# Blocked attention with one score pass: queries on partitions, exponentials turned by TensorE, divisors as extra value columns

## What is computed

```python
# x = x + att(layernorm(x)); 16 heads of 8 features, blocks of 32 tokens
qkv = (x @ Wqkv.T)                      # 128 -> 3 * 128
q, k = rope(q), rope(k)
att = einsum('bhnqd,bhnkd->bhnqk', qb, kb) * 8 ** -0.5   # within a block of 32 only
att = where(causal, att, min)
att = softmax(att, axis=-1)
out = einsum('bhnqk,bhnkd->bhnqd', att, vb)
return out.reshape(...) @ Wout.T
```

## Time and profile before

| | |
|---|---|
| time of the runs | 3553.87 us median of 3 (3552.51 to 3564.93) |
| span of the profiled execution | 3553.8 us, its own time within 0.1 us of the median |
| TensorE busy | 2772.3 us, 78% |
| VectorE busy | 2182.0 us, 61% |
| ScalarE busy | 1794.2 us, 50% |
| GpSimd busy | 1143.1 us, 32% |
| mean granted clock of TensorE | 0.844 of 2.4 GHz |

### The profile page before, as it was taken

The page is one execution under the profiler, slowest core; times in us unless marked ns, Lnnn a source line. Parts: engine busy times, 40 slices in busy tenths (PEclk is TensorE's granted clock), DMA queues, the critical chain, the costliest instruction groups (busy, mean ns, idle before and its releaser), DMA issues. The chain is left out here.

```text
span 3553.8 us, 75251 instructions
## 1 busy us (share of the span) xinstructions
PE 2772.3 (78%) x28949; PEld 2193.2 (62%) x28949; DVE 2182.0 (61%) x8175; ACT 1794.2 (50%) x3540; POOL 1143.1 (32%) x1567
## 2 busy tenths in 40 slices
PE   6788887659588585359489999999999668548886
PEld 3466664447366454246378888888888545336665
DVE  6566647753357733444477777777777663464546
ACT  5244435224234332236368988889897444313332
POOL 3200004440642613656552222222222265650002
PEclk9699978779678787669799999999999778757776
DMA  9200000015100143115100000000000014310000
GB/s 278 80 3 3 3 2 1 18 49 143 46 20 2 36 118 100 44 57 179 43 19 12 8 5 12 12 1 12 12 1 1 5 39 140 104 29 3 4 4 25
DMA packets 134083, 148.41 MB, mean 42 GB/s; under 512 B 14817, under 2 KB 109922, under 8 KB 133730
## 3 DMA queue, kind: packets, MB, share of 16 engines
q1 hardware_dynamic: 106306, 71.13, 6.9%
q0 software_dynamic: 27424, 72.48, 6.8%
HBM read 77.63 MB, written 65.93 MB: 40 GB/s over the span
## 5 line engine op out<-in xcount | busy, mean ns | idle before, releaser
L202 PE MATMUL bank<-ident,xn 128*128 128x128 f32 x320 | 72.6, 368 | 327.2 <-DVE xn L190 168.3
L2766 POOL TENSOR_SCALAR shared_floats<-shared_floats 128x2 f32<-128x2 f32 x256 | 57.2, 224 | 720.0 <-DVE shared_floats L2757 719.9
L2688 PE MATMUL bank<-layer,shared_floats 128*128 128x128 f32 x2048 | 278.2, 280 | 0.0
L1798 PE MATMUL bank<-shared_floats 32*128 32x32 f32 (+4 forms) x2048 | 222.1, 344 | 62.7 <-DVE shared_floats L1943 35.1
L202 PEld LDWEIGHTS bank<-ident,xn 128*128 128x128 f32 x320 | 47.6, 185 | 346.2 <-DVE xn L190 172.2
L2045 ACT ACTIVATE shared_floats<-bank 128x480 f32<-128x480 f32 (+2 forms) x256 | 104.5, 460 | 306.9 <-PE bank L1819 306.8
L2688 PEld LDWEIGHTS bank<-layer,shared_floats 128*128 128x128 f32 x2048 | 256.5, 197 | 0.0
L2999 ACT ACTIVATE shared_floats<-bank,layer 128x256 f32<-128x256 f32 x512 | 210.1, 470 | 89.8 <-PE bank L2675 89.7
L2675 PE MATMUL bank<-shared_floats,layer 128*128 128x256 f32 x1024 | 242.9, 380 | 0.0
L1943 DVE TENSOR_REDUCE shared_floats<-bank 128x2 f32<-128x256 f32 (+3 forms) x320 | 134.8, 471 | 170.5 <-PE bank L1812 169.8
L1805 PE MATMUL bank<-shared_floats 32*128 32x32 f32 (+7 forms) x2048 | 232.2, 339 | 4.5 <-ACT shared_floats L2045 2.4
(11 more groups left out here) (355 smaller groups left out, 8552.3 us busy)
## 6 DMA issues: line engine op xcount, KB each, us to landing
bins<-zero SPq DMA_DIRECT2D x1, 18176.0 KB, 86.6
shared_floats<-bins SPq DMA_DIRECT2D x32, 320.0 KB, 4.2
results<-shared_floats SPq DMA_DIRECT2D x32, 320.0 KB, 3.5
expert_weights<-in_dram_experts SPq DMA_DIRECT2D x32, 312.0 KB, 3.1
layer<-in_dram_layers SPq DMA_DIRECT2D x8, 902.0 KB, 4.7
bins<-zero SPq DMA_DIRECT2D x1, 5760.0 KB, 22.4
bins<-xn,f_bin_row POOLq DMA_INDIRECT x256
results<-results,result_rows POOLq DMA_INDIRECT x128
```

Source lines behind the costliest of these rows:

```text
L1798: T.matmul(k.bank[4 + r % 2][:, at_a:at_a + wide_a], q_heads[rows32(r), blk * P:(blk + 1) * P], kk[rows32(r), half_a * BK + begin_a:half_a ...
L2688: m = T.matmul(to, hidden[:, n * S + t * P:n * S + (t + 1) * P], w["w2"][:, tile(n)], start=False, stop=(n == NF - 1), skip_group_check=True)
```

## The change

`att3_*` no longer share code with `att0_*`. There is one score pass: the queries of a block are the stationary operand (32 rows by 32 columns), the spread keys the moving one (128 columns, four heads by 32 keys), so a batch's scores for all 16 heads lie with queries on partitions in two banks (`pair_of_banks`, banks 4 and 5 or 6 and 7 by turns). VectorE takes the maximum of every 32 columns and subtracts it (`shift`), ScalarE takes the exponentials of 1024 columns, TensorE turns them with eight transposes into the same two banks (`turn_exps`), ScalarE copies them (`copy_turned`), and `weigh` uses them as the stationary operand (32 columns) with the values as the moving one, 36 columns: the last four hold ones for the head's own keys (`same_head`), so that the divisor comes out of the same matmul. The result has tokens on partitions and is turned by two transposes (`turn_att`, `copy_att`) before the output projection. Queries are no longer spread. Chunks are normalised two ahead. Keys are projected before queries. The eight banks become slices of one PSUM tensor.

```diff
-BLOCKED_A = [[(b, b * BK, b * BK + BK) for b in range(BLOCKS)]]
-BLOCKED_ORDER = [("score", 0, 0), ("project", 0, 0), ("heads", 0, 0), ("weigh", 0, 3), ("divide", 0, 3), ("stats", 0, 0),
...
-BLOCKED = Softmax("L3_wqkvT", BLOCKED_A, BLOCKED_B, 4, 3, BLOCKED_ORDER, CAUSAL)
+V_WIDTH = BK + 4
+def pair_of_banks(k, n):
+    first = 4 + n % 2 * 2
+    return k.banks[:, first * CH:(first + 2) * CH]
+def heads_at(r, t):
+    return slice(r % 2 * CH + r // 2 * S + t * P, r % 2 * CH + r // 2 * S + (t + 1) * P)
 def att3_tensor(k, s):
-    softmax_tensor(k, s, BLOCKED)
+    def score(n):
+        c, to = n // 2, pair_of_banks(k, n)
+        q, _, k_heads, _ = att3_buffers(k, c)
...
+        for bank in range(2):
+            T.matmul(tiles(to[:, bank * CH:(bank + 1) * CH], BK), k.ident_bf[:, :],
+                     k.w["masks"][:, MASKS["ahead_a"]][:, 0:BK].unsqueeze(1).broadcast_to([P, CH // BK, BK]),
+                     start=True, stop=False, skip_group_check=True)
+        for rows in ((0, 1), (2, 3)):
+            if rows[0]:
+                T.wait_ge(k.sem("at_max"), LEFT["at_max"] + n + 1)
+            for t in range(QT):
+                for b in range(4):
+                    blk = n % 2 * BLOCKS + t * 4 + b
+                    for r in rows:
+                        m = T.matmul(to[rows32(b), heads_at(r, t)], q[rows32(r), blk * BK:(blk + 1) * BK],
+                                     k_heads[rows32(r), blk * P:(blk + 1) * P], start=False, stop=True, skip_group_check=True)
+            m.then_inc(k.sem("at_scored_a" if rows[0] else "at_max"), 1)
+    def turn_exps(n):
...
+        for r in range(4):
+            for t in range(QT):
+                m = T.transpose(to[:, heads_at(r, t)], exps[:, heads_at(r, t)], k.ident[:, :])
+    def weigh(n):
...
+        for t in range(QT):
+            for r in range(4):
+                for b in range(4):
+                    at = ((n % 2 * BLOCKS + t * 4 + b) * 4 + r) * V_WIDTH
+                    m = T.matmul(k.bank[3][rows32(b), (t * 4 + r) * V_WIDTH:(t * 4 + r + 1) * V_WIDTH],
+                                 turned_exps[:, heads_at(r, t)][:, b * BK:(b + 1) * BK],
+                                 v_heads[:, at:at + V_WIDTH], start=True, stop=True, skip_group_check=True)
...
+    for n in range(B + 1):
+        c, odd = n // 2, n % 2
+        on, more = n < B, c + 1 < NC
+        if on:
+            score(n)
+        if on and not odd:
+            values(c, 0)
+            values(c, 1)
+        if n:
+            weigh(n - 1)
+        if on and not odd:
+            values(c, 2)
+            values(c, 3)
+            if more:
+                ln_turn(k, s, c + 1)
+        if on and odd and more:
+            project(c + 1, 0)
+        if on:
+            turn_exps(n)
+        if n:
+            turn_att(n - 1)
+        if on and not odd and more:
+            project(c + 1, 1)
+        if n:
+            project_out(n - 1)
 def att3_vector(k, s):
-    softmax_vector(k, s, BLOCKED)
+    def shift(n):
...
+        v.count(V.tensor_reduce(tops[:, :], scores, AX.X, ALU.max))
...
+        V.tensor_tensor(tiles(exps[:, :], BK), scores, tops[:, :].unsqueeze(2).broadcast_to([P, 4 * BLOCKS, BK]),
+                        ALU.subtract).then_inc(k.sem("at_shifts_made"), 1)
+    def divide(n):
...
+        v.count(V.reciprocal(by_heads, sums[:, :, BK:V_WIDTH]))
...
+    for n in range(B + 1):
...
+        if on:
+            shift(n)
+        if n:
+            divide(n - 1)
+        if on and not odd and c + 2 < NC:
+            ln_stats(k, s, c + 2)
+        if on and not odd and more:
+            turn_heads(c + 1, 1)
+        if on and odd and more:
+            turn_heads(c + 1, 0)
+        if on and odd and c + 2 < NC:
+            ln_apply(k, s, c + 2)
+        if n:
+            add_out(n - 1)
 def att3_scalar(k, s):
-    softmax_scalar(k, s, BLOCKED)
+    for n in range(B + 1):
...
+        if on and not odd:
+            copy_values(c, 0)
+            copy_values(c, 1)
+        if on:
+            exps(n)
+        if on and not odd:
+            copy_values(c, 2)
+            copy_values(c, 3)
+            if more:
+                ln_copy(k, s, c + 1)
+        if on and odd and more:
+            mask_heads(c + 1)
+        if on:
+            copy_turned(n)
+        if n:
+            copy_att(n - 1)
```

More of the change, by code:

```diff
@@ L46, in tiles @@
     return ap.rearrange("p (t d) -> p t d", d=inner)
-SHARED = {"f0_": 0, "at_": 1, "l1_": 2, "f1_": 3, "e_": 3, "g_": 3, "e2_": 5, "f3_": 6}
+SHARED = {"f0_": 0, "at_": 1, "l1_": 2, "f1_": 3, "e_": 3, "g_": 3, "e2_": 5, "f3_": 6, "b3_": 7}
 SHARED_FLOATS = 19900
@@ L70, in __init__ @@
         self.x = self.sb("x", [P, N // P * D])
-        self.bank = [nc.alloc_psum_tensor(f"bank{n}", [P, CH], F32) for n in range(8)]
+        self.banks = nc.alloc_psum_tensor("banks", [P, 8 * CH], F32)
+        self.bank = [self.banks[:, n * CH:(n + 1) * CH] for n in range(8)]
     def sb(self, name, shape, dtype=F32):
@@ L2092 @@
                 ("score", 5, 0), ("add", 0, 2), ("weigh", 0, 1), ("values", 3, 0), ("copy values", 3, 0)]
-BLOCKED_A = [[(b, b * BK, b * BK + BK) for b in range(BLOCKS)]]
-BLOCKED_ORDER = [("score", 0, 0), ("project", 0, 0), ("heads", 0, 0), ("weigh", 0, 3), ("divide", 0, 3), ("stats", 0, 0),
-                 ("values", 0, 0), ("copy values", 0, 0),
-                 ("score", 1, 0), ("shifts", 0, 1), ("copy shifts", 0, 1), ("project", 1, 0), ("heads", 1, 0),
-                 ("values", 1, 0), ("copy values", 1, 0), ("out", 0, 3), ("apply", 0, 0), ("add", 0, 3), ("parts", 0, 0),
-                 ("values", 2, 0), ("copy values", 2, 0), ("turn", 0, 0), ("copy turned", 0, 0),
-                 ("q heads", 0, 0), ("k heads", 0, 0), ("values", 3, 0), ("copy values", 3, 0)]
-BLOCKED_B = BLOCKED_A
 CAUSAL = Softmax("L0_wqkvT", CAUSAL_A, CAUSAL_B, 8, 2, CAUSAL_ORDER)
-BLOCKED = Softmax("L3_wqkvT", BLOCKED_A, BLOCKED_B, 4, 3, BLOCKED_ORDER, CAUSAL)
 def att0_tensor(k, s):
@@ L2118, in att0_gpsimd, with att3_buffers @@
     softmax_gpsimd(k, s, CAUSAL)
-def att3_tensor(k, s):
-    softmax_tensor(k, s, BLOCKED)
-def att3_vector(k, s):
-    softmax_vector(k, s, BLOCKED)
-def att3_scalar(k, s):
-    softmax_scalar(k, s, BLOCKED)
+V_WIDTH = BK + 4
[4 more added lines that the diff above has]
+    return slice(r % 2 * CH + r // 2 * S + t * P, r % 2 * CH + r // 2 * S + (t + 1) * P)
+def att3_buffers(k, c):
+    return [k.sb(f"b3_{name}{c % 2}", [P, width]) for name, width in
+            (("q", CH), ("k", CH), ("k_heads", 4 * CH), ("v_heads", CBLOCKS * 4 * V_WIDTH))]
@@ new lines, in att3_exps, with att3_turned @@
+def att3_exps(k, n):
+    return k.sb(f"b3_exps{n % 2}", [P, 4 * S])
+def att3_turned(k, n):
+    return k.sb(f"b3_turned{n % 2}", [P, 4 * S])
+LEFT = {"at_qk": 2 * NC, "at_projected": 2 * NC, "at_k_heads": NC, "at_q_heads": NC, "at_values": 4 * NC, "at_v_heads": 4 * NC,
+        "at_scored_a": B * CAUSAL.slots, "at_scored_b": B * CAUSAL.slots, "at_max": B * CAUSAL.units, "at_exps": B * CAUSAL.units,
+        "at_parts": B, "at_shifts_made": B, "at_shifts": B, "at_weighed": B * CAUSAL.nr, "at_att": B, "at_out": B, "at_added": NC}
@@ L2133, in att3_gpsimd @@
 def att3_gpsimd(k, s):
-    softmax_gpsimd(k, s, BLOCKED)
+    for c in range(NC):
+        ln_rstd(k, s, c)
 def products_before(s):
```

143 lines of the change are left out of this document (added).

## The result

| | before | changed |
|---|---|---|
| time of the runs, same chip | 3553.19 us median of 4 (3545.47 to 3564.93) | 3458.34 us median of 4 (3453.49 to 3462.07) |
| span of the profiled execution | 3553.8 us | 3458.0 us (its own time 3459.31) |
| ratio | | 0.9735, 95% interval 0.9704 to 0.9766 |
| last addition of the stage ahead begins | 3189.25 | 3175.87 |
| from there to the end of the last addition of the blocked attention | 307.8 us | 225.3 us |

The kernel became 2.65% faster. I had forecast 3487 with a range of 3455 to 3526: direction and range held, but the median lies only 3.3 us inside the lower bound, and the move was about 95 us where I had 66.6.

What follows compares the result with a forecast made beforehand. TensorE's order of work was taken to set the pace. Eight chunks of 27.6 us are 221, with the ends 223 against 289.6, so 3553.8 - 66.6 = 3487 us, range 3455 to 3526.

Steps and rivals of the forecast that it cites:

- The clock of 0.80: TensorE's granted clock over the changed blocked attention, taken a little over the 0.77 before; each 0.1 worth some 18 us.
- the hidden fills: Stage head: second normalising and two fills of ones (0.42 each) fit VectorE's 5.7 us wait; uncovered about 4.8 us.
- The ends: First and last chunk of the stage: +1 cold start, -4 nothing to prepare, +5 for the serial tail.
- full-clock walk: One chunk's chain across engines, even then odd batch, job durations laid end to end at full clock: 24.0 us.
- the factor 0.97: Correction on the chunk time, because the method's sum for the old kernel was 3% high (33.8 against 32.7 us).
- the signs that I named: Profile after: score batch 2 to 2.5 us, eight transposes 1.3, opening transposes 27 to 28 apart, clock about 0.8, among others.
- The mixing of the clocks: Chunk time from 24.0 us at full and 36.3 at half clock, weighted 0.6 and 0.4: 27.8 us.
- The check of the method: Old kernel's chunk summed from row prices, 27.8 and 45.2 us, mixed at clock 0.77: 33.8 against 32.7 measured.
- The clock stays up: Rival: odd-batch waits too short to lower the clock; chunk 24.0 us, stage 194, kernel 3458; chance 0.15.
- The clock goes down instead: Rival: new transposes do not hold the clock, about 0.6; chunk 32.6 us, kernel 3527, all cold 3553; chance 0.10.
- Handovers cost more: Rival: passing between engines adds 2 us wait per batch; chunk 31.5 us, stage 254, kernel 3518; chance 0.12.
- The small tiles do not run side by side: Rival: score matmuls on 32x32 tiles pass serially, 7 us a batch; chunk about 42, kernel 3602; chance 0.05.

Runs made afterwards that it cites:

- fill_mm: Changed kernel plus 13 f32 matmuls whose results nobody reads in each odd batch's two TensorE waits, except the last; 3320.90 us, ratio 0.9684 to before.
- changed_again: The changed kernel, nothing edited, profiled once more on another chip; 3334.36 us, ratio 0.9736 to the kernel before.
- fill_transposes: Changed kernel plus unused transposes, 7 and 16, in the odd batch's two TensorE waits; 3315.39 us, ratio 0.9682 to the kernel before.
- scores_twice: Changed kernel with every score matmul issued twice onto the same place; 3356.73 us, ratio 0.9792 to the kernel before.

## Why the prediction was right, and where its size was off

**What held.** The pace is TensorE's order of work, before and after, with ScalarE's order in the two waits of an odd batch. These waits came out as walked, 1.15 and 2.31 for 0.85 and 2.3, and idle time was 5.2 us a chunk where the walk's 1.3, 0.85 and 2.3 with the 0.7 of other idle make 5.15. The odd batch of 10.4 us for the 10.5 of the walk is in part chance: its output projection ran at half clock, 0.46 us dearer from start to start, and in fill_mm the same batch at full clock takes 9.9. The clock of 0.80 was measured as 0.80, but I had chosen it, a little over the 0.77 of before, and not worked it out; one stretch of 10 us at half clock in each chunk is nothing that the prediction had. VectorE's 1.22, ScalarE's 1.02, the hidden fills and the unchanged head held (the head by 1 us). The ends came to 208.2 - 8 x 25.5 = +4.2 for my +2.

**The step that was mis-sized** is the full-clock walk, "So 24.0 a chunk". fill_mm runs the same order at full clock in 21.9. (The 0.7 and the factor 0.97 left 24.0 where it was.) The walk laid durations end to end, but in the rows the next job starts before the duration of the one ahead is over. The chunk of fill_mm from 3153.91 to 3175.82 closes: its jobs last 18.7 us where the walk's sum is 19.6, its waits (with the fill in them) 4.9 where the walk has 4.45, and 14 overlaps of 0.06 to 0.18 us take 1.7 off, which the walk put at nothing: 21.9. Opening transposes, turned exponentials, turned result, key projection and output projection I had walked in 5.0 us (8.5 to 13.5); in fill_mm they take 3.74 from the first's start to the masks that follow, 1.3 of the 2.1. The eight transposes show it best: "twice the L202 row" made 1.3, where the row is 1.04 and the next job starts after 0.87. A score batch is 1.92 at full clock and 3.26 at half for my 2.2 and 3.7. So of the signs that I named, three missed, mostly for this reason: the score batch under 2 us, the eight transposes at 1.04 instead of 1.3, and the opening transposes 24.9 to 25.8 us apart instead of 27 to 28.

**The mixing of the clocks** was right once its input is: 40% of the time at half clock and my ratio of 36.3 to 24.0, applied to 21.9, give 1 / (0.6/21.9 + 0.4/33.1) = 25.3, and 25.5 was measured. (No run has a whole chunk at half clock, so the 33.1 is not measured itself.) The check of the method on the kernel before could not find the fault, since there the same durations were summed and a factor of 0.97 taken for the rest. Eight chunks at 2.1 are 17 us, less 2 for the ends: 208.2 for the 223 of the forecast.

**The rest of the miss.** In the first pair the profiles differ by 95.8 us where I had 66.6, 29.2 more. Of these 14.8 are the chunks and ends just named, 1.0 is the head, and 13.4 lie ahead of the stage, outside my sum, with their cause open. Elsewhere these 13.4 are absent and the gain beside changed_again is nevertheless 93, since in its other executions the kernel before took 6 to 10 us more in the stage, at a clock of 0.71, than in the one execution that gave me 289.6. That both come to about the same is chance as far as the runs show.

**The rivals.** *The clock stays up* gave 3458, and 3458.34 was measured. It is wrong all the same: its chunk was 24.0 at full clock, the trace has 25.5 at 0.80. The time alone would have confirmed it. With the true full-clock chunk its state is that of fill_mm, 25 us better. *The clock goes down instead* fell with the 0.80 and with fill_transposes. *Handovers cost more* fell with 5.2 us of idle time a chunk. *The small tiles do not run side by side* fell with 1.46 us for both halves (7 in series) and with 0.92 us for 32 matmuls more.

The sixteen tiles of the Trainium skill ("TensorE: Matmul & The Clock Gate", Part 3, measured speedup vs the span model) led to an estimate of 0.55 us a half. Here two halves take 1.46 us, with a wait of TensorE on itself of 0.13 between them, so 0.67 each: nearer to the 0.7 worked out from the rows than to the 0.55.

## What to carry to other kernels

When a chain is walked with durations from a timeline, step from start to start, and use the whole duration only where the next job waits for the result: 14 joints of 0.06 to 0.18 us made 1.7 us of a chunk of 24. A short wait on TensorE can cost more than itself, since the jobs behind it may run at half clock; look at which jobs follow each wait, and move work of the engine waited for out of the way first, or fill the wait with matmuls that nobody reads. Take the base of a forecast from more than one execution where the clock changes level within the stage, and when the measured time meets a rival's number, look whether its mechanism is in the trace before believing it.

## What the runs showed of the hardware

- Filling idle time of TensorE with unused work made the kernel faster: 13 f32 matmuls of 128 columns a chunk took the stage from 225.8 to 200.9 us, with the clock at 0.99 for 0.81; 23 transposes did the same, at 1.00.
- In each of the six chunks of the changed kernel one stretch of about 10 us at half clock began during or right behind the odd batch's second wait (3216.3 to 3226.6 in the windows above). In one chunk of scores_twice a wait of 2.21 us in the same place left the clock at 1.00.
- With the second wait at 1.16 us instead of 2.31 the clock stayed up in some chunks and fell in others of the same execution (20.8 and 24.4 us).
- An f32 matmul on a 32x32 tile with 128 columns, eight tiles in use, adds 29 ns at full clock (0.92 us for 32) and 53 at half.
- A reciprocal of 32 columns took 0.35 us, against 1.76 for 256 in the earlier trace rows.
- The same stage of the kernel before took 307.8, 313.9 and 317.6 us in three executions, at a clock of 0.77, 0.71 and 0.71 over six chunks.
